# Five of sixteen key and value steps projected in earlier stages, a key scratch with all 96 rows of each head, stores issued by the sync engine

## The chip, the cores and the metric

The kernel runs on one core of a Trainium2 chip. Its engines are PE (TensorE, the matrix engine, with PEld for its weight loads), DVE (VectorE), ACT (ScalarE), POOL (GpSimd) and SP (SyncE, which here only issues transfers). Each engine runs its own list of instructions in order and waits on semaphores for the others. The metric is the time of one execution in microseconds, as the median over several runs.

## The reference

The program is a small perceiver of two layers over a residual x of 8 x 32 = 256 tokens by 256 channels, with a context of 8 x 512 = 4096 tokens. Cut to what matters:

```python
def fq(x, axis):                       # int8 rounding in f32
    s = max(max(|x|, axis) / 127, 1e-8)
    return clip(round(x / s), -127, 127) * s

x = x + masked_attention(layernorm(x), ctx, mask)       # keys and values are ctx itself
x = x + scan(layernorm(x))                              # state space scan, 64 states
x = x + moe(layernorm(x), experts=64, top=6)            # grouped choice, and a shared expert

q = (layernorm(x) @ Wq + bq) / 4                        # 16 heads of 16 channels
k, v = split(ctx @ Wkv + bkv)                           # 4096 tokens each
q, k = fq(q, axis=channel of head), fq(k, axis=channel of head)
v = fq(v, axis=token)                                   # one scale per channel, over all tokens
p = softmax(q @ k.T)                                    # then rounded to 255 steps of its maximum
x = x + (p @ v) @ Wp + bp

x = x + gated convolution and MLP; x = x + moe(layernorm(x), experts=16, top=4)
```

## The kernel before

The program is a sequence of seven stages, each a block of the five engines' programs with a barrier behind it: first attention (`xattn0_stage`), scan, first mixture of experts (`moe0_stage`), keys and values (`kv_stage`), heads (`xattn1_stage`), convolution and MLP (`conv_stage`), second mixture (`moe_stage`). Within a stage the order of each engine is the order in which the code is written; there is no scheduler. What one engine does is released to another by a semaphore (`wait_ge`, `then_inc`).

**Keys and values.** The 4096 context tokens are taken in 16 steps of 256 (`STEPS`, `KPS` = 2 chunks of 128 tokens). For step m PE makes two halves, keys and values: each four f32 matmuls of 128x256 (L1683) and two short ones (L1685) that add the bias, held in three bf16 parts. DVE quantizes the keys per head in five operations (L1505 to L1512). ACT and POOL split the f32 result exactly into three bf16 parts (L1620, L1577, L1624, L1580). Two steps later PE turns the 3 x 2 x 2 blocks of 128x128 (L1698), ACT copies the turned keys from PSUM to one of two buffers `k_kT` (L1610) and issues their store to a scratch in HBM (L1614). ACT also copies the values (L1599) and their absolute values (L1602), of which DVE keeps a running maximum (L1540), which POOL reduces over the partitions at the end. SP loads the context of each step into one of two slots as soon as PE has projected the step two back (L1366), and at the end begins the loads of the keys of heads 0 and 1. The queries are projected, quantized and split in the same stage, between the steps.

The copy of turned keys waits for the store that last left the same buffer:

```python
def copy_turned(m):
    act.wait_ge(kT_psum, m + 1)
    if m >= 2:
        act.wait_ge(kT_stored[m % 2], m // 2 * 16)
```

**The scratch and the heads.** The product of queries and keys is made exactly from six products of parts (`PRODUCTS`), so each head's keys stand as 6 x 16 = 96 rows in SBUF (`kst`). The scratch holds the three parts once (3 x 256 rows). Each head's 96 rows are read from it by six transfers of 16 rows, since a part that is in several products is read several times (`load_keys`, L1373). Heads 0 and 1 are loaded in pieces: the first 12 steps, the steps 12 to 14 (`LATE`), and the last step straight from SBUF (`last_keys`). In the head stage PE multiplies (L2068), DVE takes the maximum (L1913), ACT the exponential (L2009), POOL rounds (L1895), and PE turns and multiplies by the values (L2095, L2111).

**The stages around.** In the first attention PE turns the normalized tokens, makes the scores in two halves (L281), turns the exponentials (L287) and multiplies by the context (L296). The first mixture gathers the tokens of four experts at a time with matmuls (L1033), runs them through (L1048, L1060, L1069, L1081) and adds them back (L1091), 16 groups in a pipelined loop; four slots hold the experts' weights, two of them (`w0_early`) loaded during the first attention. There the bias of keys and values is split into parts too (L959, L853). `keep_warm` (L122) is a helper of matmuls whose result nobody reads.

## Time and profile before

| | us |
|---|---|
| runs | 713.3, 715.14, 716.4 |
| median | 715.14 |
| profiled execution | 715.68 |
| its span | 713.6 |
| first attention | 33.5 |
| scan | 133.3 |
| first mixture | 118.4 |
| keys and values | 88.3 |
| heads | 213.9 |
| convolution and second mixture | 126.2 |

The profiled execution is 715.68 us long, of which the span of instructions is 713.6 us. Over the span PE is busy for 86%, DVE 67%, ACT 55% and POOL 37% of the time, and the mean granted clock of TensorE is 0.916 of full. These shares are averages over stages with different limits, so each stage is read by itself, in the windows of the rows below. A row of the timeline has the start, the duration and the engine; what stands in square brackets is how long the engine had been idle and what released it. Of transfers the issue is on the queue of an engine (SPq, ACTq), and the landing is told from the issue.

### The profile page before, as it was taken

To read this page: it belongs to the slowest core of one execution; us is meant where nothing else is said; L and a number is where in the kernel's file an instruction comes from. 1 tells how busy PE (TensorE), PEld (TensorE's weight loads), DVE (VectorE), ACT (ScalarE), POOL (GpSimd) and SP (SyncE) were. 2 spreads that over 40 slices of the span, in tenths; PEclk is the share of its full clock that TensorE was granted. 3 is DMA by queue.
4 is the path that set the end of the run, shared out by engine and by line. 5 is a ranking of instruction groups with operands and counts; after the bars stand their busy time and mean duration, and the time that the engine had idled before them with its cause. 6 is when DMAs were issued, how large, how long until landed. Compare 5 with 4: busy or idle time off the path is not lost. (4 is left out here: it accounts for less than half of the span.)

```text
span 713.6 us, 12686 instructions
## 1 busy us (share of the span) xinstructions
PE 612.9 (86%) x4694; PEld 403.5 (57%) x4694; DVE 480.9 (67%) x762; ACT 393.8 (55%) x759; POOL 331.7 (46%) x263
## 2 busy tenths in 40 slices
PE   3767999994899999989965788888898879989996
PEld 1333445443677776877741445554555566657775
DVE  3358999995543323778977799999899945333222
ACT  1237965533222222568867799999899943122221
POOL 1039999992111110244634778888788920000000
PEclk9988999999799999999995598889768879999999
DMA  8918300005166660144463969797898639700000
GB/s 345 337 49 326 125 0 1 0 0 177 59 200 198 200 200 1 56 123 142 132 177 97 191 127 164 150 169 142 160 153 143 126 62 410 300 1 1 0 0 15
DMA packets 97802, 93.84 MB, mean 132 GB/s; under 512 B 70673, under 2 KB 88657, under 8 KB 93585
## 3 DMA queue, kind: packets, MB, share of 16 engines
q1 hardware_dynamic: 85072, 86.72, 45.6%
q10 hardware_dynamic: 12672, 6.36, 3.1%
q8 instruction: 36, 0.59, 0.3%
q14 instruction: 22, 0.17, 0.1%
HBM read 69.56 MB, written 6.62 MB: 107 GB/s over the span
## 5 line engine op out<-in xcount | busy, mean ns | idle before, releaser
L1913 DVE TENSOR_REDUCE d_nmax<-d_psum 128x1 f32<-128x1024 f32 x128 | 152.1, 1214 | 7.9 <-PE d_psum L2068 7.7
L2068 PE MATMUL d_psum<-kst,qT 96*128 96x512 bf16 x256 | 97.2, 476 | 31.3 <-ACT d_e L2009 11.8
L426 POOL TENSOR_TENSOR b_h<-b_h,b_cb 128x1024 f32<-128x1024 f32 x32 | 87.7, 2740 | 6.8 <-DVE b_h L476 6.0
L1895 POOL TENSOR_SCALAR d_rounded<-d_e,d_lift 128x1024 f16<-128x1024 f32 x64 | 72.4, 1132 | 21.2 <-ACT d_lift L2013 14.4
L2009 ACT ACTIVATE d_e<-d_psum,d_nmax 128x1024 f32<-128x1024 f32 x64 | 71.3, 1119 | 17.4 <-DVE d_nmax L1913 16.7
L1895 POOL TENSOR_SCALAR d_rounded<-w_early,d_lift 128x1024 f16<-128x1024 f32 x62 | 70.1, 1131 | 17.3 <-ACT d_lift L2013 13.1
L476 DVE TENSOR_TENSOR_SCAN b_h<-b_dA,b_psum 128x1024 f32<-128x1024 f32 x32 | 73.2, 2286 | 2.5 <-ACT b_dA L531 2.0
L531 ACT ACTIVATE b_dA<-b_dtT,b_A 128x248 f32<-128x248 f32 x128 | 53.7, 490 | 33.1 <-DVE b_h L476 28.1
L2009 ACT ACTIVATE w_early<-d_psum,d_nmax 128x1024 f32<-128x1024 f32 x64 | 71.4, 1121 | 0.1
L1683 PE MATMUL k_psum<-k_wkv,k_ctxT 128*128 128x256 f32 x256 | 64.1, 381 | 1.4 <-PEq L812 1.4
L2095 PEld LDWEIGHTS d_psum<-d_ident_f,d_rounded 128*128 128x128 f16 x512 | 43.2, 119 | 32.6 <-issue 20.1
L587 PE MATMUL b_psum<-b_bdiag,b_dtx 128*128 128x512 f32 x128 | 60.2, 594 | 0.8 <-DVE b_h L476 0.8
L2095 PE MATMUL d_psum<-d_ident_f,d_rounded 128*128 128x128 f16 x512 | 50.4, 257 | 6.2 <-ACT d_probsT L2021 3.1
L2068 PEld LDWEIGHTS d_psum<-kst,qT 96*128 96x128 bf16 x256 | 19.8, 110 | 59.6 <-ACT d_e L2009 20.9
L1683 PEld LDWEIGHTS k_psum<-k_wkv,k_ctxT 128*128 128x128 f32 x256 | 43.5, 190 | 11.1 <-issue 1.8
L2111 PEld LDWEIGHTS d_psum<-d_vh,d_probsT 128*128 128x128 f16 x1024 | 43.5, 98 | 9.7 <-issue 5.5
L847 POOL TENSOR_TENSOR c_pick_weighed<-c_pick,c_w 128x384 f32<-128x384 bf16 x16 | 13.4, 838 | 76.2 <-PE c_psum L1069 70.2
L2111 PE MATMUL d_psum<-d_vh,d_probsT 128*128 128x16 f16 x1024 | 43.9, 171 | 2.3 <-issue 1.6
L608 PE MATMUL b_psum<-b_h,ident 128*128 128x256 f32 x128 | 36.1, 404 | 6.9 <-DVE b_h L483 4.4
L608 PEld LDWEIGHTS b_psum<-b_h,ident 128*128 128x128 f32 x128 | 21.8, 189 | 33.8 <-DVE b_h L483 32.2
L1272 PE MATMUL f_psum<-w,f_xnT 128*128 (+1 forms) x128 | 40.5, 459 | 0.0
L883 DVE TENSOR_TENSOR c_a<-c_silu,c_psum 128x192 f32<-128x192 f32 x16 | 5.7, 355 | 51.0 <-ACT c_silu L947 51.0
(398 smaller groups left out, 1177.2 us busy)
## 6 DMA issues: line engine op xcount, KB each, us to landing
kst<-kT_scratch SPq DMA_DIRECT2D x84, 128.0 KB, 3.0
w<-in_w SPq DMA_DIRECT2D x8, 1088.0 KB, 19.3
b_cb<-c_scratch SPq DMA_DIRECT2D x4, 2048.0 KB, 7.1
w_early<-in_w0gu SPq DMA_DIRECT2D x8, 768.0 KB, 5.0
w_late<-in_w0gu SPq DMA_DIRECT2D x8, 768.0 KB, 4.9
kT_scratch<-k_kT ACTq DMA_DIRECT2D x15, 384.0 KB, 2.7
a_ctxT<-in_ctxT SPq DMA_DIRECT2D x2, 2048.0 KB, 12.2
a_ctx<-in_ctx SPq DMA_DIRECT2D x2, 2048.0 KB, 20.7
```

The lines of the kernel that those rows point to most:

```text
L426: nc.gpsimd.tensor_tensor(hv, hv, cv, ALU.mult).then_inc(hc_ready, 1)
L476: nc.vector.tensor_tensor_scan(h[s][:, :], dA[s % 2][:, :], ps[:, 2 * (s % 2):2 * (s % 2) + 2, :] .rearrange("p a b -> p (a b)"), 0.0, ALU ...
L531: nc.scalar.activation(out[:, :, j, :, 1:L], src, ACT.Exp, scale=A[:, c, n * NT + j:n * NT + j + 1]).then_inc(dA_ready, 1)
L587: last = nc.tensor.matmul(ps[:, 2 * (s % 2) + t, :], dtx[:, t, c * P:(c + 1) * P], bdiag[t][:, n * NT:n * NT + NT, :], start=True, stop=True)
L608: last = nc.tensor.matmul(ps[:, 4 + c, 0:T], ident[:, :], hv[:, j], start=False, stop=False, skip_group_check=True)
L1683: nc.tensor.matmul(psum_kv(m, part)[:, j, :], cT[m % 2][:, k, j * P:(j + 1) * P], wkv[:, k, cols], start=(k == 0), stop=False)
L1895: nc.gpsimd.tensor_scalar(tile_of(r, j), e[j], lift[t][:, f:f + 1], HALF_ULP_ONE, ALU.mult, ALU.add).then_inc(r_ready, 1)
L1913: nc.vector.tensor_reduce(nm[:, t, m:m + 1, f:f + 1], quarter(m, j).unsqueeze(1), AX.X, ALU.max, negate=True).then_inc(nm_ready, 1)
L2009: nc.scalar.activation(e[j].unsqueeze(1), quarter(m, j).unsqueeze(1), ACT.Exp, bias=nm[:, t, m:m + 1, f], accum_out=zp[:, t, m:m + 1, f]). ...
L2068: last = nc.tensor.matmul(quarter(m, j)[:, b * 512:(b + 1) * 512], qT[0:QROWS, m:m + 1, t * P:(t + 1) * P], kst[m % 2][0:QROWS, at:at + 51 ...
L2095: last = nc.tensor.transpose(turn_tile(m, j)[:, b * P:(b + 1) * P], tile_of(r, j)[:, b * P:(b + 1) * P], ident16[:, :])
L2111: last = nc.tensor.matmul(out, pT[m % 2][:, t, b, :], vh[m % 2][:, b, :], start=(b == 0), stop=(b == NKC - 1 and t not in BY_DMA))
```

## The change

**Projected ahead.** Steps 0 to 4 of keys and values (ten halves) are projected before their stage: five halves in the first attention and five in the first mixture. ACT copies each from PSUM to SBUF (`keep_half`). To that end the weights `wkv` are loaded second in the program, the context of these steps ahead of the rest, and the bias is split at the very start of the first attention, by POOL, ACT and DVE. In the loop of the first mixture DVE quantizes the five key steps, ACT and POOL split them, and DVE takes the values' maximum so far. The weights of the first mixture's experts are now all loaded at its own start, since the memory of the two early slots (`spare`) holds the early keys, values and `wkv`.

**The key and value stage** has 11 steps (5 to 15), three slots for the context and five for the split parts. `TURNS` says which turns stand in which pass of the loop; those of the early steps are doubled up with the later ones. The absolute copies of the values are gone; DVE takes the maximum from the values themselves, every second step, and POOL's reduction over the partitions moves to the head stage, with the value scale after it.

**The scratch** holds all 96 rows of each head, so the parts are written as often as they are used: a step's store is six transfers (768 KB) in place of one (384 KB), and SP issues them. A head's keys are one transfer of 96 rows (768 KB).

**Smaller edits.** Fewer `keep_warm` matmuls (28 to 19 and 12 to 3 in the convolution stage, 17 to 14 in the second mixture, 5 to 0 in the first, whose place the projections take); in the convolution stage the products are released one by one, the two kinds of silu alternate, and the gates follow two convolutions behind.

```diff
+EARLY_PROJECTED = 5
+FIRST_HALVES = ((0, 0), (0, 1), (1, 0), (1, 1), (2, 0))
+SECOND_HALVES = ((2, 1), (3, 0), (3, 1), (4, 0), (4, 1))
...
+def keep_half(nc, act, g, n, bank):
...
+    act.wait_ge(g["early_psum"], n + 1)
+    nc.scalar.activation(dst, bank.rearrange("p (c n) -> p c n", n=D), ACT.Copy).then_inc(g["early_read"], 1)
...
                 step = Steps(dve, chain)
+                dve.wait_ge(bkv_in, 16)
+                for q in range(K_PARTS):
+                    src = ([bkv] + bias_rest)[q]
+                    nc.vector.tensor_copy(bias_part[q][:, :], src[:, :]).then_inc(bias_part_ready, 1)
+                    if q < K_PARTS - 1:
+                        dve.wait_ge(bias_part_ready, q + 1)
+                        step(nc.vector.tensor_tensor(bias_rest[q][:, :], src[:, :], bias_part[q][:, :], ALU.subtract))
                 dve.wait_ge(g["x_in"], 16)
                 ln.vector(dve, step, xn, x, xn_ready)
...
+STORED_ROWS = ((0, 3), (3, 2), (5, 1))
+STORED = 16 * len(STORED_ROWS) * KC
...
+def store_keys(queue, g, src, done, cols):
+
+    dst = g["kT_store"][:, :, :, cols]
+    parts = src[:, :, :].rearrange("p (q k) n -> p q k n", q=K_PARTS)
+    for first, count in STORED_ROWS:
+        for k in range(KC):
+            queue.dma_start(dst[:, first:first + count, k, :], parts[:, 0:count, k, :]).then_inc(done, 16)
+
+
+def load_keys(queue, d, dst, done, head, cols):
+
+    queue.dma_start(dst[0:QROWS, cols], d["kT_scratch"][head * QROWS:(head + 1) * QROWS, cols]).then_inc(done, 16)
...
+TURNS = ((0,), (), (1, 2), (3, 4), (5,), (6, 7), (8, 9), (10,), (11,), (12,), (13,))
+QUERY_PARTS = (5, 7, 9)
...
             @block.sync
             def _(sp):
-                for m in range(2, STEPS):
-                    sp.wait_ge(v_psum, m - 1)
-                    load_context(sp, d, g, m)
+                def store(m):
+                    sp.wait_ge(kT_ready, m + 1)
+                    store_keys(sp, g, kT[slot(m)], kT_stored[slot(m)], slice(m * KEYS, (m + 1) * KEYS))
+
+                for i in range(STEPS - FIRST):
+                    m = FIRST + CTX_SLOTS - 1 + i
+                    if FIRST + CTX_SLOTS <= m < STEPS:
+                        sp.wait_ge(v_psum, nth(m - CTX_SLOTS))
+                    if m < STEPS:
+                        load_context(sp, d, g, m)
+                    if i:
+                        for u in TURNS[i - 1]:
+                            store(u)
...
                 for h in range(2):
                     load_keys(sp, d, g["kst"][h], g["k_early"][h], h, EARLY)
+                for m in (LAST - 1, LAST):
+                    store(m)
...
                 def copy_turned(m):
 
                     act.wait_ge(kT_psum, m + 1)
                     if m >= 2:
-                        act.wait_ge(kT_stored[m % 2], m // 2 * 16)
+                        act.wait_ge(kT_stored[m % 2], m // 2 * STORED)
...
+                for i in range(STEPS - FIRST):
+                    if i:
+                        copy_values(FIRST + i - 1)
+                    split0(FIRST + i)
+                    for m in TURNS[i][0:1]:
+                        copy_turned(m)
+                    split1(FIRST + i)
+                    for m in TURNS[i][1:]:
+                        copy_turned(m)
+                    if i in QUERY_PARTS:
+                        query_part(QUERY_PARTS.index(i))
+                copy_values(LAST)
...
+                for i in range(STEPS - FIRST):
+                    keys(FIRST + i)
...
+                    for m in TURNS[i]:
+                        turn(m)
+                    if i:
+                        values(FIRST + i - 1)
+                values(LAST)
                 turn(LAST - 1)
```

How the instructions stand now is shown at three places. First SP in the key and value stage. Before, `k_v_psum` (the values of a step are in PSUM) releases one context load after the other, and behind the last the loads of the keys:

```order
L812 UNCONDITIONAL_BRANCH
L1480 UNCONDITIONAL_BRANCH [waits barrier_Pool_Activation_PE_DVE_SP_release]
L1366 DMA k_ctxT<-in_ctxT 128x2x256 [waits k_v_psum] x14
L1373 DMA kst<-kT_scratch 16x3072 [waits kT_stored1,kT_stored0]
L1373 DMA kst<-kT_scratch 16x3072 x11
```

Now, in the passes of the loop around the turns 3 and 4, the stores of two steps stand between two context loads (`k_kT_ready` is the copy of turned keys):

```order
L1541 DMA k_ctxT<-in_ctxT 128x2x256 [waits k_v_psum]
L1555 DMA kT_scratch<-k_kT 128x3x256 [waits k_kT_ready]
L1555 DMA kT_scratch<-k_kT 128x3x256
L1555 DMA kT_scratch<-k_kT 128x2x256 x2
L1555 DMA kT_scratch<-k_kT 128x256 x2
L1555 DMA kT_scratch<-k_kT 128x3x256 [waits k_kT_ready]
L1555 DMA kT_scratch<-k_kT 128x3x256
L1555 DMA kT_scratch<-k_kT 128x2x256 x2
L1555 DMA kT_scratch<-k_kT 128x256 x2
L1541 DMA k_ctxT<-in_ctxT 128x2x256 [waits k_v_psum]
```

The stores have moved from ACT to SP, behind a context load and its wait for the values. The second place is ACT in one pass of the same stage. Before:

```order
L1620 ACTIVATE k_parts<-k_kq 128x512 [waits k_kT_psum,k_kq_ready]
L1599 ACTIVATE v<-k_psum 128x512 [waits k_v_psum]
L1602 ACTIVATE k_v_abs<-k_psum 128x512 [waits k_vrun_ready]
L1610 ACTIVATE k_kT<-k_psum 128x1536 [waits kT_stored0,k_kT_psum]
L1624 ACTIVATE k_parts<-k_rest 128x512 [waits k_rest_ready]
L1614 DMA kT_scratch<-k_kT 128x6x256 [waits k_kT_ready]
L1620 ACTIVATE k_parts<-k_kq 128x512 [waits k_kT_psum,k_kq_ready]
```

And now one and a half passes, of which the first has two copies of turned keys (L1810), each with its wait for a store of its own buffer (`kT_stored0`, `kT_stored1`):

```order
L1803 ACTIVATE v<-k_psum 128x512 [waits k_v_psum]
L1816 ACTIVATE k_parts<-k_kq 128x512 [waits k_kq_ready]
L1810 ACTIVATE k_kT<-k_psum 128x1536 [waits kT_stored1,k_kT_psum]
L1820 ACTIVATE k_parts<-k_rest 128x512 [waits k_rest_ready]
L1810 ACTIVATE k_kT<-k_psum 128x1536 [waits kT_stored0,k_kT_psum]
L1803 ACTIVATE v<-k_psum 128x512 [waits k_v_psum]
L1816 ACTIVATE k_parts<-k_kq 128x512 [waits k_kq_ready]
L1810 ACTIVATE k_kT<-k_psum 128x1536 [waits kT_stored1,k_kT_psum]
L1820 ACTIVATE k_parts<-k_rest 128x512 [waits k_rest_ready]
```

The issue of the store and the absolute copy are gone, and a second copy of turned keys has come into the pass. The third place is PE at the program's start. Before, it turns the normalized tokens (`a_xn`) and makes the scores:

```order
L114 MATMUL a_psum<-ident,a_xn 128x128 [waits a_xn_ready,constants_ready]
L114 MATMUL a_psum<-ident,a_xn 128x128 x3
L281 MATMUL a_psum<-a_ctxT,a_xnT 32x512 [waits a_ctxT_in0,a_xnT_ready]
L281 MATMUL a_psum<-a_ctxT,a_xnT 32x512 x7
L281 MATMUL a_psum<-a_ctxT,a_xnT 32x512 [waits a_ctxT_in1]
L281 MATMUL a_psum<-a_ctxT,a_xnT 32x512 x7
```

Now a half of keys stands ahead of the transposes and two halves behind them (L137 and L138, with `spare` the memory of `wkv`):

```order
L137 MATMUL a_psum<-spare,a_ctxT 128x256 [waits k_wkv_in,a_first_ctxT_in0,k_bias_ready,constants_ready]
L137 MATMUL a_psum<-spare,a_ctxT 128x256
L138 MATMUL a_psum<-k_bias_rows,ones_bf 128x256
L137 MATMUL a_psum<-spare,a_ctxT 128x256 x2
L138 MATMUL a_psum<-k_bias_rows,ones_bf 128x256
L120 MATMUL a_psum<-ident,a_xn 128x128 [waits a_xn_ready]
L120 MATMUL a_psum<-ident,a_xn 128x128 x3
L137 MATMUL a_psum<-spare,a_ctxT 128x256 x2
L138 MATMUL a_psum<-k_bias_rows,ones_bf 128x256
L137 MATMUL a_psum<-spare,a_ctxT 128x256 x2
L138 MATMUL a_psum<-k_bias_rows,ones_bf 128x256
L137 MATMUL a_psum<-spare,a_ctxT 128x256 [waits k_early_read,a_first_ctxT_in1]
```

The scores (L281 before) come behind three halves, and the first instruction waits for the bias parts (`k_bias_ready`) and the weights (`k_wkv_in`) too.

## Rows read from the trace of the kernel before

**Rows 1.** Windows by stage: busy us of each engine (instructions), granted clock, DMA share, GB/s

```profile
core 0: us, PE busy (x) PEld busy (x) DVE busy (x) ACT busy (x) POOL busy (x), PEclk, DMA share, GB/s
0.00:33.50 33.50, 17.75 (x108) 7.73 (x109) 10.73 (x26) 6.10 (x11) 1.90 (x13) 0.95 0.93 350
33.50:166.80 133.30, 115.27 (x353) 58.86 (x353) 115.38 (x111) 75.94 (x190) 106.92 (x44) 0.96 0.19 71
166.80:285.20 118.40, 108.86 (x844) 80.90 (x844) 49.30 (x137) 29.28 (x65) 19.28 (x29) 0.96 0.50 156
285.20:373.50 88.30, 79.50 (x544) 63.69 (x544) 71.39 (x111) 64.39 (x87) 40.62 (x34) 0.99 0.43 124
373.50:587.40 213.90, 174.66 (x2332) 109.00 (x2333) 191.69 (x269) 186.34 (x328) 162.87 (x143) 0.78 0.77 142
587.40:713.60 126.20, 116.90 (x513) 83.29 (x513) 42.40 (x109) 31.73 (x81) 0.11 (x1) 1.00 0.25 103
```

**Rows 2.** Groups of the key and value stage: busy, mean ns, idle before

```profile
L1683 PE MATMUL k_psum<-k_wkv,k_ctxT 128*128 128x256 f32 x256 | 64.1, 381 | 1.4 <-PEq L812 1.4
L1698 PE MATMUL k_psum<-ident_bf,k_parts 128*128 128x128 bf16 x192 | 13.4, 219 | 6.5 <-POOL k_parts L1580 4.4 <-DVE k_parts L1566 1.9
L1610 ACT ACTIVATE k_kT<-k_psum 128x1536 bf16<-128x1536 bf16 x14 | 20.3, 1452 | 2.1 <-PE k_psum L1698 2.1
L1638 ACT ACTIVATE qs<-k_q_rest 128x1024 bf16<-128x1024 f32 x1 | 2.0, 1987 | 0.0
```

**Rows 3.** Timeline of PE, one step: start, duration, instruction

```profile
358.75 0.84 PE L1698 MATMUL k_psum<-ident_bf,k_parts 128*128 128x128 bf16 x12
363.39 0.83 PE L1698 MATMUL k_psum<-ident_bf,k_parts 128*128 128x128 bf16 x12
```

**Rows 4.** Store and context load by source line: duration ns, issue to landing

```profile
L1614 ACTq DMA_DIRECT2D kT_scratch<-k_kT x15: 366/366/406, 301.7 to 369.8; - x15
DMA to landing us min/median/max: 2.7/2.7/3.3
L1366 SPq DMA_DIRECT2D k_ctxT<-in_ctxT x16: 539/540/634, 171.8 to 353.6; - x16
```

**Rows 5.** DMA issues, first attention: KB, us to landing

```profile
b_cols<-in_cols SPq DMA_DIRECT2D x1, 4.0 KB, 2.4
```

**Rows 6.** Timeline of PE in the first mixture

```profile
179.23 0.23 PE L1010 MATMUL c_psum<-c_selb,before_bf 128*128 128x64 bf16 x1 [4.86 <-DVE c_selb L708]
183.59 2.08 PE L1033 MATMUL c_psum<-c_pick,c_xn_part 128*128 128x192 bf16 x12 [0.30 <-ACT c_gatheredT L941]
188.72 1.16 PE L1033 MATMUL c_psum<-c_pick,c_xn_part 128*128 128x192 bf16 x12
```

**Rows 7.** Windows in the first mixture and in the first attention

```profile
177.00:178.00 1.00, 0.00 (x0) 0.00 (x0) 0.86 (x5) 0.00 (x0) 0.00 (x0) 0.50 1.08 363
24.00:25.50 1.50, 1.50 (x10) 0.66 (x8) 0.00 (x0) 0.00 (x0) 0.00 (x0) 0.50 0.90 372
186.00:277.00 91.00, 91.00 (x748) 67.91 (x744) 33.16 (x70) 21.89 (x53) 13.83 (x16) 0.99 0.50 157
```

**Rows 8.** Timeline in the first attention, DVE and PE

```profile
15.84 0.69 DVE L242 SCALAR_TENSOR_TENSOR a_scores<-a_psum,a_mask 128x512 f32<-128x512 f32 x1 [6.54 <-PE a_psum L281]
22.57 9.80 PE L296 MATMUL a_psum<-a_ctx,a_expT 128*32 128x256 f32 x64
```

**Rows 9.** Timeline of PE where the heads begin

```profile
379.99 1.04 PE L2068 MATMUL d_psum<-kst,qT 96*128 96x512 bf16 x4 [1.87 <-DMA kst<-kT_scratch]
403.52 1.89 PE L2068 MATMUL d_psum<-kst,qT 96*128 96x512 bf16 x4 [3.79 <-DMA kst<-kT_scratch]
```

**Rows 10.** Timeline in the convolution stage, DVE and PE

```profile
591.95 0.69 DVE L2161 TENSOR_TENSOR e_hn<-e_y,e_ss 128x512 f32<-128x512 f32 x1
593.47 0.60 PE L114 MATMUL e_psum<-ident,e_hn 128*128 128x128 f32 x4
602.90 0.43 DVE L2229 TENSOR_TENSOR e_gated<-e_sx,e_sz 128x256 f32<-128x256 f32 x1 [2.03 <-ACT e_sx L2282]
```

580 lines of the change are left out of this document (346 added, 234 removed).

## The prediction

> **What bounds the kernel now.** I read the views in this order. First the windows by stage [rows 1]: the span of 713.6 us falls into seven stages, with a barrier between each two. PE is busy for 79.5 of the 88.3 us of the key and value stage (285.2 to 373.5) and for 108.86 of 118.4 us of the first mixture of experts. The head stage (373.5 to 587.4) is different: DVE is busy 191.69 and ACT 186.34 of its 213.9 us, PE 174.66. So work that moves off PE in the key stage shortens that stage, the same work laid on PE in the mixture lengthens it, and the heads go faster only where they wait for keys.
>
> Second, the groups of instructions of the key stage [rows 2] and one of its steps on PE [rows 3]. In a step PE does eight f32 matmuls of 0.38 us for keys and values, some short ones for their bias, and one turn. Turn to turn that takes 363.39 - 358.75 = 4.64 us: one turn of three key parts at 0.84 us and two halves (keys, values) at (4.64 - 0.84) / 2 = 1.90 us each. Third, its queues [rows 4]: a store of a step's turned keys (384 KB, one transfer, issued by ACT in 0.37 us) lands 2.7 us later, and SP needs 0.54 us to issue a context load. Fourth, PE's idle stretches and the granted clock. Last, the small waits at the edges of the other stages.
>
> **Key and value stage.** Five of 16 steps go. What goes on PE is ten halves; their five turns stay: 5 x (4.64 - 0.84) = 19.0 us. Two things come back. The last step's keys are stored by six issues of SP at 0.54 us in place of one of 0.37 us at the stage's end: +2.9. Three query copies of ACT, up to 2.0 us each [rows 2], now lie in a stage of 11 steps with as many 1.45 us copies of turned keys as before; I put 1.0 us of them on the path. That leaves -15.1 us, if nothing new is waited for.
>
> Something is. The turned keys have two buffers, so the copy of step m waits until the store of step m-2 has landed. Before, ACT issued that store right behind its copy, a whole step ahead of need. Now SP issues it, and in front of it in SP's program stands a context load that waits for the values of the same loop pass. That event is also the one with which ACT begins the pass in which it makes the next copy. So for passes whose stores were not issued earlier (the four that end with turns 3 and 4, 5, 6 and 7, 8 and 9, each followed by the turn that needs them), one loop from values to values is: context issue 0.54, store, copy 1.45, turn 0.84, values 1.90. In words: PE's turn m waits for the copy of m-2, that for the store of m-4, that for SP, and SP for PE's values.
>
> The store is now six issues of 64 to 192 KB, 768 KB in all. No row shows six such stores. From above: six at SP's 0.54 us, the last landing after the 2.7 us of a 384 KB store, 5 x 0.54 + 2.7 = 5.4 us. From below: a pitch of ACT's 0.37 us and a landing of 2.4 us, that of a 4 KB load [rows 5], 5 x 0.37 + 2.4 = 4.2 us. I take 4.5, nearer to the low end, since the issue of a store is the 0.37 us row, and the last piece is small. The loop is then 0.54 + 4.5 + 1.45 + 0.84 + 1.90 = 9.2 us. PE's own work in it is 4.64 us with one turn and 4.64 + 0.84 = 5.48 us with two: two passes of either kind, so 2 x 4.6 + 2 x 3.7 = +16.6 us (bounds +15.4 and +20.2 with the store at 4.2 and 5.4).
>
> The Trainium skill, "DMA: Bandwidth & Descriptors", section "Anatomy of one DMA", says that the fixed part of a DMA, about 2.0 us, is mostly the receipt of the write, and is the longest where the target is HBM. By that rule as an estimate, the six transfers would share one fixed part, 2.0 us plus the issue of the last, and the loop would be some 0.4 us shorter. The page is for the path of another queue, and no row of this trace splits a landing in two.
>
> Each of the four passes now holds a stretch in which PE waits: from the end of the keys (1.90 us into the loop) to the copy (6.5 us in), 4.6 us. The rows at 179 us show what such a stretch does: PE had been idle for 4.86 us when it started at 179.23 [rows 6], and the granted clock was 0.50 already at 177 us [rows 7]; that is the 1.2 GHz level. At 183.59 twelve gather matmuls still took 2.08 us, and at 188.72 twelve took 1.16 us. So after an idle of 4.86 us the halved clock outlives it by at least 6.4 us of work (179.23 to 185.67). In the loop, turn and values (2.74 us) would take 5.48 us. If all four passes lose this it is +11.0 us, if none it is 0. I take +6.5, since the first stall starts at full clock and PE fills part of the rest with slower keys that nothing waits for.
>
> The Trainium skill, "TensorE: Matmul & The Clock Gate", section "HAM oscillation — how this bites in real kernels", tells of loops in which a wait longer than the tile's work throttles the engine again in each tile, so that each starts cold. By that rule the whole +11.0 would be paid, and it speaks against this change; [rows 6, 7] agree with the drop behind one idle stretch, while no row of this trace shows it four times in a row.
>
> Sum of the stage: -15.1 + 16.6 + 6.5 = +8.0 us. Its bounds are -15.1 and, with the long store and all four at the half rate, -15.1 + 20.2 + 11.0 = +16.1.
>
> **First attention.** Five halves come in, 5 x 1.90 = 9.5 us of PE. Ahead of them stands a chain that did not exist: a small load (2.4 us to land, [rows 5]), then on DVE three casts and two subtractions of 512 columns, 0.69 us for such an operation [rows 8], and three ACT copies of a row. DVE does them before the LayerNorm, and PE starts behind them. That moves the first scores by about 3 us. Most of the other halves lie in waits that PE has there, for loads, exponentials and copies. Against it: the values matmuls of this stage, 9.80 us for 64 from 22.57 [rows 8], run partly at a granted clock of 0.50 (24.0 to 25.5, [rows 7]), and a PE that has worked in the gaps before them can win up to 2 us. I take +2.0 (bounds 0 and +5).
>
> **First mixture.** It is PE bound: 91.0 of 91.0 us busy from 186 to 277 [rows 7]. The half in its loop costs its full 1.9 us, and the two in front of the transposes delay the logits by about 0.8. Two halves go into the idle stretch of 4.86 us [rows 6], behind which the clock was halved: two gathers of 2.08 us against 1.16 give 1.8 us back, and slower matmuls beside them another 0.7. DVE is busy in 33.16, ACT in 21.89 and POOL in 13.83 of those 91 us, so quantizing, splitting and subtracting five steps hides there. Rounded up for the zeros matmul that now stands behind the shared expert: +0.6 (bounds -1.5 and +3).
>
> **Heads.** PE waited 1.87 us at 379.99 and 3.79 us at 403.52 for keys [rows 9]; the second is the load of head 2, issued as six transfers behind the many small ones of heads 0 and 1. With one transfer per head SP is free some 5 us earlier, and most of the 3.79 goes. The first is partly replaced by the wait of heads 0 and 1 for stores that now end later. The value scale moves into head 0. I take -4 (bounds -6, which is nearly all of both waits and a little later, and +1). The other heads run at the pace of DVE and do not change.
>
> **Convolution and last mixture.** In before, the normalized rows were ready at 591.95 + 0.69 = 592.64, but warming matmuls held PE until 593.47: -0.8. DVE waited 2.03 us until 602.90 for the first gate [rows 10], and the convolutions now run two ahead of the gates; half of it counts, as PE waits for gates too: -1.0. With fewer warming matmuls the clock may fall in the gap: +0.6. Together -1.2 (bounds -3, +2); fewer warming matmuls at the last stage's start, -0.4.
>
> **Sum.** The scan does not change. 715.68 + 2.0 + 0.6 + 8.0 - 4.0 - 1.2 - 0.4 = 720.7 us against the profiled execution. That one lies 0.54 us above the median of the runs, 715.14 us, so I forecast 720.
>
> **Rivals.** (A) The store comes back sooner than SP's rows say. Its six parts are small, and the place is the same loop: if the last lands 2.0 us after SP goes on, the loop is 6.7 us, the stall 2 x 2.1 + 2 x 1.2 = 6.6 us, PE's idle stretches are 2.1 us, and I let the clock stay at 2.4 GHz. The stage is then -15.1 + 6.6 = -8.5 and the time 720 - 8.0 - 8.5 = 703.5 us. It decides from a store below 3 us. For it: 384 KB in one transfer lands in 2.7. Against it: 768 KB and six issues. 0.17; faster. (B) The stores are waited for as I say, but the clock does not fall: 720 - 6.5 = 713.5 us. For it: each stall has work on both sides. Against it: [rows 6]. 0.25. (C) Forecast: 720, own range 715 to 726: 0.43. (D) The clock stays at half from the first stall to the end of the stage, keys too: the +11.0 in full and 4 x 1.9 us for keys where PE no longer idles enough, of which I put half on the path: 720 + 4.5 + 3.8 = 728, up to 733 with the long store. 0.15. That the change does not remove the five steps is no case: the order shows it.
>
> **Numbers.** A change of 0.5% (3.6 us) is what a measurement of this kernel can tell from none, so "same" is 711.6 to 718.7. Faster: all of A, 0.10 of B (gains in the heads at their bound), 0.03 of C: 0.30. Same: 0.13 of B, 0.06 of C: 0.19. Slower: the rest of C, 0.02 of B and D: 0.51. The range 703 to 729 leaves out 0.08 below and 0.08 above.
>
> **What the profile after would show.** The stage of keys and values 92 to 100 us long, with four waits of PE's turns of 4 to 5 us each ended by ACT's copy, whose own wait is ended by a DMA of the scratch; a granted clock of 0.50 behind them. First attention 35 to 36 us, first mixture 118 to 120 us without an idle stretch of PE above 3 us, heads about 210 us. I am wrong if the copies of turned keys wait less than 2 us for stores, or if those waits are there and the clock stays at 1.00.

## The result and the profile after

| | before | after |
|---|---|---|
| median of the runs | 715.0 (4 runs) | 736.04 (4 runs) |
| span of the profiled execution | 713.6 | 734.8 |
| first attention | 33.5 | 36.2 |
| scan | 133.3 | 133.3 |
| first mixture | 118.4 | 119.7 |
| keys and values | 88.3 | 105.5 |
| heads | 213.9 | 213.6 |
| convolution | 42.2 | 42.4 |
| second mixture | 84.0 | 84.1 |

The changed kernel is slower: 1.0302 times the time before, with a 95% interval of 1.0248 to 1.0357. The forecast was 720 us with a range up to 729; the sign was right, the size was not. The windows of the kernel after, of the key and value stage and of the heads, answer to [rows 1] (busy us of each engine with instructions, granted clock, DMA share, GB/s):

```profile
core 0: us, PE busy (x) PEld busy (x) DVE busy (x) ACT busy (x) POOL busy (x), PEclk, DMA share, GB/s
...
289.20:394.70 105.50, 70.22 (x443) 55.65 (x443) 49.49 (x89) 48.23 (x56) 25.82 (x22) 0.84 0.53 150
394.70:608.30 213.60, 176.50 (x2332) 113.99 (x2332) 193.26 (x271) 187.06 (x327) 163.56 (x144) 0.77 0.78 142
```

PE did 70.22 us of work in the key and value stage, 9.3 less than before, and the stage became 17.2 us longer. The granted clock fell there from 0.99 to 0.84. The heads did not become shorter. Most of the loss beyond the forecast lies in these two stages.

PE's timeline in the pass with turn 5 is the first of four of its kind, and shows what takes the place of [rows 3]:

```profile
313.58 0.27 PE L138 MATMUL k_psum<-k_bias_rows,ones_bf 96*128 96x256 bf16 x1
319.17 1.44 PE L1883 MATMUL k_psum<-ident_bf,k_parts 128*128 128x128 bf16 x12 [5.32 <-ACT k_kT L1810]
320.40 2.02 PE L137 MATMUL k_psum<-spare,k_ctxT 128*128 128x256 f32 x4
```

PE ends the keys at 313.85 us and idles for 5.32 us; then the turn takes 1.44 us (0.84 before) and the first four matmuls of the values 2.02 us (1.03 at full clock). ACT in the same pass shows what PE waited for:

```profile
311.94 0.60 ACT L1803 ACTIVATE v<-k_psum 128x512 f32<-128x512 f32 x1 [2.94 <-PE k_psum L138]
...
317.57 1.45 ACT L1810 ACTIVATE k_kT<-k_psum 128x1536 bf16<-128x1536 bf16 x1 [4.52 <-DMA kT_scratch<-k_kT]
```

ACT copies the values as soon as they are there, splits, and then waits until the store of two steps before has landed, 5.6 us after the values (311.94 to 317.57). The six transfers of that store took 5.0 us from the first issue (312.52) to the landing of the last, which came 2.1 us behind its own issue. Over the stage the waits of ACT and of PE in that circle add up (engine and line waited for, us in total, times, longest):

```profile
ACT k_kT L1810 <- DMA kT_scratch<-k_kT: 22.8, 7, 4.6
PE k_psum L1883 <- ACT k_kT L1810: 21.3, 7, 5.4
```

The second half of the loss is at the end of the stage. PE's last turn, the last copy of turned keys (by DVE) and SP's stores there:

```profile
383.22 0.84 PE L1883 MATMUL k_psum<-ident_bf,k_parts 128*128 128x128 bf16 x12
```

```profile
385.12 0.96 DVE L1756 COPY k_kT_last<-k_psum 128x1536 bf16<-128x1536 bf16 x1
```

```profile
312.52 6.73 SPq L1555 DMA_DIRECT2D kT_scratch<-k_kT  x12
...
368.89 16.28 SPq L1555 DMA_DIRECT2D kT_scratch<-k_kT  x24
...
386.16 4.35 SPq L1555 DMA_DIRECT2D kT_scratch<-k_kT  x6
390.56 3.76 SPq L1555 DMA_DIRECT2D kT_scratch<-k_kT_last  x6
```

PE's last turn had ended at 384.06 us, 10.85 us before PE's first instruction in the next stage, and the last copy at 386.08; SP issues stores up to 394.3. In the kernel before the last copy of turned keys ended at 372.3 and the stage at 373.5, 1.2 us later; here it is 8.6 us later, for a queue. PE's last turn there, 2.2 us before the end of the stage:

```profile
370.46 0.84 PE L1698 MATMUL k_psum<-ident_bf,k_parts 128*128 128x128 bf16 x12 [1.89 <-DVE k_parts L1566]
```

This is a matter of the end and not of the whole stage, as SP's own waits show (for copies of turned keys, from 288 us to the end of the stage):

```profile
SPq L1555 <- ACT k_kT L1810: 3.0, 2, 1.9
```

The row of 24 stores from 368.89 us hides these two waits: SP had caught up, and issued the stores of steps 12 and 13 as soon as ACT had copied their keys (the latter at 381.86). Behind that copy stand 20 issues, the six stores of each of the steps 13, 14 and 15 and two loads of keys, and they take 12.5 us, while PE needs only 2.2 more. The six stores of a step, by their source line (answer to [rows 4]):

```profile
L1555 SPq DMA_DIRECT2D kT_scratch<-k_kT x90: 370/493/915, 299.9 to 390.0; - x90
...
DMA to landing us min/median/max: 1.6/2.4/6.5
```

The median issue takes 0.49 us, but they follow each other at 0.56 to 0.62 us where SP doesn't wait (6.73 us for 12, 12.5 for the last 20), where the prediction had 0.54, and 0.37 as its lower bound.

### The profile page after: what moved, and what is told of

Its sections match the earlier page's. It is cut to its first block and busy times, and to the rows that moved or that the text cites. A ratio compares the mean times of both kernels' runs of the same rounds, so it can differ in the third digit from the quotient of the medians.

```text
span 734.8 us, 12653 instructions
## 1 busy us (share of the span) xinstructions
PE 618.0 (84%) x4667; PEld 413.8 (56%) x4667; DVE 481.4 (66%) x776; ACT 389.0 (53%) x746; POOL 328.3 (45%) x263
## 5 line engine op out<-in xcount | busy, mean ns | idle before, releaser
L2261 PE MATMUL d_psum<-kst,qT 96*128 96x512 bf16 x256 | 98.9, 484 | 40.9 <-ACT d_e L2202 18.8
L2089 POOL TENSOR_SCALAR d_rounded<-spare,d_lift 128x1024 f16<-128x1024 f32 x62 | 70.1, 1131 | 18.3 <-ACT d_lift L2206 14.1
L2202 ACT ACTIVATE spare<-d_psum,d_nmax 128x1024 f32<-128x1024 f32 x64 | 71.3, 1118 | 1.6 <-DVE d_nmax L2109 1.6
L2288 PEld LDWEIGHTS d_psum<-d_ident_f,d_rounded 128*128 128x128 f16 x512 | 48.9, 129 | 31.5 <-issue 23.7
L2288 PE MATMUL d_psum<-d_ident_f,d_rounded 128*128 128x128 f16 x512 | 55.5, 274 | 3.4 <-POOL d_rounded L2089 2.2
L137 PE MATMUL k_psum<-spare,k_ctxT 128*128 128x256 f32 x176 | 52.2, 432 | 1.4 <-PEq L931 1.4
L2304 PEld LDWEIGHTS d_psum<-d_vh,d_probsT 128*128 128x128 f16 x1024 | 42.4, 96 | 7.6 <-issue 2.1
L137 PEld LDWEIGHTS k_psum<-spare,k_ctxT 128*128 128x128 f32 x176 | 35.1, 221 | 10.3 <-issue 4.0
L1445 PE MATMUL f_psum<-w,f_xnT 128*128 (+1 forms) x128 | 40.5, 460 | 0.0
L1377 DVE TENSOR_TENSOR f_prod<-f_silu,f_psum 128x352 f32<-128x352 f32 x16 | 8.3, 522 | 42.2 <-ACT f_silu L1416 42.2
```

The source lines that it names most:

```text
L137: nc.tensor.matmul(out[:, j, :], ctxT[:, k, j * P:(j + 1) * P], g["wkv"][:, k, cols], start=(k == 0), stop=False)
L1445: last = nc.tensor.matmul(GU[t][u][:, 0:width], xnT[:, k, t * P:(t + 1) * P], parts[u][:, k, :], start=(k == 0), stop=(k == KC - 1))
L2089: nc.gpsimd.tensor_scalar(tile_of(r, j), e[j], lift[t][:, f:f + 1], HALF_ULP_ONE, ALU.mult, ALU.add).then_inc(r_ready, 1)
L2202: nc.scalar.activation(e[j].unsqueeze(1), quarter(m, j).unsqueeze(1), ACT.Exp, bias=nm[:, t, m:m + 1, f], accum_out=zp[:, t, m:m + 1, f]). ...
L2261: last = nc.tensor.matmul(quarter(m, j)[:, b * 512:(b + 1) * 512], qT[0:QROWS, m:m + 1, t * P:(t + 1) * P], kst[m % 2][0:QROWS, at:at + 51 ...
L2288: last = nc.tensor.transpose(turn_tile(m, j)[:, b * P:(b + 1) * P], tile_of(r, j)[:, b * P:(b + 1) * P], ident16[:, :])
```

## The experiments

All are compared with runs of the kernel before on the same chip, so that each ratio has its own time before (715.0 to 716.6 us). The stage lengths are those of the profiled execution of each.

| run | time | ratio to before (95%) | keys, values | heads |
|---|---|---|---|---|
| changed kernel | 736.0 | 1.030 (1.025 to 1.036) | 105.5 | 213.6 |
| stores ahead of the context wait | 712.5 | 0.993 (0.991 to 0.996) | 81.8 | 214.0 |
| four buffers | 710.9 | 0.995 (0.992 to 0.997) | 82.2 | 212.3 |
| projected ahead, scratch as before | 696.5 | 0.972 (0.969 to 0.975) | 70.1 | 213.6 |
| scratch alone, on the kernel before | 716.8 | 1.000 (0.997 to 1.003) | 96.4 | 207.1 |
| PE kept warm in the stalls | 727.9 | 1.019 (1.014 to 1.024) | 96.8 | 210.0 |
| value scale back | 728.7 | 1.019 (1.013 to 1.024) | 104.6 | 206.6 |
| convolution warmed as before | 736.1 | 1.028 (1.022 to 1.033) | 105.7 | 212.8 |
| projected ahead, with both repairs | 700.8 | 0.984 (0.976 to 0.991) | 72.2 | 212.6 |
| stores split between SP and ACT | 712.9 | 0.996 (0.992 to 0.999) | 89.5 | 209.3 |
| three loads per head | 816.0 | 1.139 (1.133 to 1.146) | 90.7 | 308.0 |
| three loads, rows outermost | 706.7 | 0.986 (0.982 to 0.989) | 71.1 | 215.1 |
| the same, scale in the heads | 707.6 | 0.986 (0.981 to 0.990) | 73.5 | 219.1 |

**Is the wait behind the values the cause?** In the changed kernel, the stores go ahead of the context wait and load of the same pass:

```diff
+                    if i:
+                        for u in TURNS[i - 1]:
+                            store(u)
                     m = FIRST + CTX_SLOTS - 1 + i
                     if FIRST + CTX_SLOTS <= m < STEPS:
                         sp.wait_ge(v_psum, nth(m - CTX_SLOTS))
                     if m < STEPS:
                         load_context(sp, d, g, m)
-                    if i:
-                        for u in TURNS[i - 1]:
-                            store(u)
```

> The changed kernel, with SP's stores of turned keys issued ahead of the context load (and its wait for the values) of the same pass, and nothing else. Theory 1 (the copy of turned keys waits for a store that stands behind a wait for PE's own values): the loop from values to values is broken. What is left is copy to store to copy, about 5.1 + 1.45 us for every second turn, and SP's 6 x 0.61 us for each store. The four idle stretches of PE of 3.8 to 5.4 us shrink to under 2 us, the clock stays at 1.00 there, the key and value stage falls from 106 to about 86 us, the time from 736 to about 716 us. Rival (the store itself is too slow for two buffers, wherever it is issued): the idle stretches stay above 3 us, the stage stays above 98 us, the time above 728 us.

712.5 us: 23.6 below the changed kernel, the stage 23.7 us shorter. The same two waits as above, in this kernel:

```profile
PE k_psum L1883 <- ACT k_kT L1810: 6.5, 7, 1.9
...
ACT k_kT L1810 <- DMA kT_scratch<-k_kT: 3.6, 2, 1.8
```

And SP's waits for copies of turned keys in it:

```profile
SPq L1555 <- ACT k_kT L1810: 16.4, 7, 7.5
```

ACT's waits for stores went from 22.8 to 3.6 us, PE's from 21.3 to 6.5. Theory 1 holds, and the time lies 3.5 us below what it expected. But the stage is 11.7 us longer than with single stores (70.1, below), though ACT's copies stall PE for no more than 1.9 us at a time. SP is not short of time over the stage: it stands idle for 16.4 us, waiting for copies. Its last such wait ends with the copy of step 13 at 360.11 us, PE's last turn ends at 362.30, and SP issues until 372.2.

**Is it the number of buffers?** The changed kernel with four buffers:

```diff
-        kT = [sb(f"k_kT{s}", [P, K_PARTS * KC, KEYS], BF16) for s in range(2)] + [g["kT_last"]]
+        kT = [sb(f"k_kT{s}", [P, K_PARTS * KC, KEYS], BF16) for s in range(4)] + [g["kT_last"]]
...
-                    if m >= 2:
-                        act.wait_ge(kT_stored[m % 2], m // 2 * STORED)
+                    if m >= 4:
+                        act.wait_ge(kT_stored[m % 4], m // 4 * STORED)
```

> The changed kernel with four buffers for turned keys in place of two, so that a copy waits for the store of four steps before. Theory 1: ACT's waits for the scratch's DMA (22.8 us) go, PE no longer idles between keys and values, the clock stays at 1.00. Theory 2 (96 store issues of SP at about 0.6 us are a bound of their own): SP then has some 64 us of issues from the first store on, so PE ends its last turn well before SP ends, and the key and value stage is about 81 us, not 73; the time is about 711 us. If SP's issues are no bound, the stage is 73 to 75 us and the time 704 us. If the wait for the buffer isn't the cause of the stalls, 736 us.

710.9 us, stage 82.2 us, as theory 1 and 2 together expected (711 and 81), and not the 704 of theory 1 alone. Either edit breaks the circle, and both end at nearly the same length of the stage, so what is left is not the circle. PE's last turn in this run, and SP behind it:

```profile
360.03 0.83 PE L1883 MATMUL k_psum<-ident_bf,k_parts 128*128 128x128 bf16 x12
```

```profile
348.34 13.88 SPq L1555 DMA_DIRECT2D kT_scratch<-k_kT  x24
...
363.25 4.22 SPq L1555 DMA_DIRECT2D kT_scratch<-k_kT  x6
367.52 3.88 SPq L1555 DMA_DIRECT2D kT_scratch<-k_kT_last  x6
371.81 2.49 SPq L1566 DMA_DIRECT2D kst<-k_kT_last  x4
```

PE has ended at 360.9 us; SP still issues stores until 371.4, and with that the stage ends. In this run SP hardly waits for copies (0.5 us in all), so by itself it fits theory 2, 96 issues as a limit of their own. The run before doesn't: with 16.4 us of idle time its stage ends no later. What the two have in common is the end: from the copy of step 13 to the last store it is 12.1 us there and 12.9 here, as it is 12.5 in the changed kernel.

**The five steps alone.** The changed kernel with the scratch of before: three parts once, one store per step by ACT, six loads per head:

```diff
-STORED = 16 * len(STORED_ROWS) * KC
+STORED = 16
...
+                    for m in TURNS[i][0:1]:
+                        store(m)
                     for m in TURNS[i][1:]:
                         copy_turned(m)
+                        store(m)
```

> The changed kernel with the scratch as before: three parts once, one store of 384 KB per step issued by ACT right behind its copy, six transfers of 16 rows for each head. The five steps stay projected ahead, and the other edits stay. Theory 1 and 2 both: no stall above 2.5 us in the key and value stage, its length about 75 us; the heads lose the single transfer, so PE waits for the keys of head 2 again (about 4 us): time about 708 us. Rival (doubled turns or the early projections themselves slow the stage): the stage stays above 85 us and the time above 718 us.

696.5 us, 0.972 of the time before, 11.5 us below what I expected. The stage's window, and PE's last turn:

```profile
288.20:358.30 70.10, 59.72 (x443) 48.19 (x443) 52.48 (x89) 48.33 (x57) 26.08 (x23) 1.00 0.48 136
```

```profile
354.51 0.84 PE L1884 MATMUL k_psum<-ident_bf,k_parts 128*128 128x128 bf16 x12 [1.08 <-DVE k_parts L1765]
```

At a full clock, 70.1 us: the five steps are worth 18.2 us, and the early halves cost 3.4 us in the first attention and nothing in the first mixture in this run. The last turn ends 67.2 us into the stage and the stage 2.9 us later; in the two kernels that broke the circle it was 71.5 and 71.3 us, and then 10.3 and 11.0. So of the 12 us between them some 4 are small waits of PE before its last turn, and 7.4 to 8 are the queue behind it. This is the fastest kernel of the study, faster than before and after.

**The scratch alone.** On the kernel before, with SP's store of a step four steps behind the context load:

```diff
                 for m in range(2, STEPS):
                     sp.wait_ge(v_psum, m - 1)
                     load_context(sp, d, g, m)
+                    if m >= 4:
+                        store(m - 4)
...
-    for j in rows:
-        queue.dma_start(dst[j:QROWS:len(PRODUCTS), cols], parts[PRODUCTS[j][1], head * HD:(head + 1) * HD, cols])\
-             .then_inc(done, 16)
+    queue.dma_start(dst[0:QROWS, cols], d["kT_scratch"][head * QROWS:(head + 1) * QROWS, cols]).then_inc(done, 16)
```

> The kernel before with only the scratch of 96 rows: SP issues six stores per step behind the context load (a step's store four steps behind the load), and a head's keys are one transfer. Here a store is issued two steps ahead of the copy that waits for it, 9.3 us, so theory 1 has no stall in the loop. Theory 2: SP needs 6 x 0.6 + 0.57 = 4.2 us of a step of 4.9, which fits, but the last four steps' stores stand at the end: stage +5 to +9 us. Heads 4 us shorter or the same. Time 716 to 721 us. Rival (the 768 KB stores themselves slow the stage, by the bytes they move): the stage is longer by 15 us or more, time above 728 us.

716.8 us, no difference from before (0.997 to 1.003). The stage is 8.1 us longer, inside the 5 to 9 expected of SP's issues, and the heads are 6.8 us shorter. Where each store is issued two steps ahead of need there is no circle: the last turn comes 1.6 us later in the stage than before, and the stage ends 8.6 us behind it in place of 2.2. From the copy of step 13 to the last store it is 12.0 us again. The single load per head pays this back.

**What does the clock cost?** Warming matmuls in front of the last turn of the four passes:

```diff
                     for m in TURNS[i]:
+                        if i in WARM and m == TURNS[i][-1]:
+                            pe.wait_ge(v_copied, i - 2)
+                            keep_warm(nc, g, ps[:, 2 * ((FIRST + i - 1) % 2) + 1, :], WARM[i])
                         turn(m)
```

> The changed kernel with 22, 19, 16 and 22 warming matmuls of PE (result read by nobody) in front of the last turn of the four passes in which PE idled 5.3, 4.6, 3.8 and 5.4 us. The stores are waited for as before; only what PE does meanwhile changes. Theory (the halved clock behind each stall costs turn and values 2.4 to 2.7 us more): the granted clock is 1.00 through the loop, a loop is 9.6 us in place of 12.0 to 12.7, the key and value stage 96 to 98 us in place of 106, the time about 727 us. Rival (the clock costs nothing, since slower matmuls only fill waits): stage and time unchanged, 736 us.

727.9 us. The four passes in the window of the changed kernel and of this one, and PE's timeline in this one:

```profile
311.90:361.00 49.10, 29.42 (x154) 22.98 (x154) 17.12 (x29) 18.55 (x21) 10.57 (x9) 0.76 0.47 134
```

```profile
312.70:353.00 40.30, 37.34 (x230) 23.72 (x230) 17.14 (x29) 17.98 (x20) 10.12 (x9) 1.00 0.57 164
```

```profile
314.47 4.91 PE L128 MATMUL k_psum<-ones_bf,ident_bf 128*128 128x512 bf16 x22
320.24 0.83 PE L1884 MATMUL k_psum<-ident_bf,k_parts 128*128 128x128 bf16 x12 [0.86 <-ACT k_kT L1811]
...
330.35 0.83 PE L1884 MATMUL k_psum<-ident_bf,k_parts 128*128 128x128 bf16 x12 [0.54 <-ACT k_kT L1811]
...
350.52 0.83 PE L1884 MATMUL k_psum<-ident_bf,k_parts 128*128 128x128 bf16 x12 [0.54 <-ACT k_kT L1811]
```

The granted clock is 1.00 in place of 0.76, the four passes take 40.3 us in place of 49.1, and the stage is 8.7 us shorter. That is the price of the clock here, 2.2 us for each of the four stalls. A pass is 10.1 us (320.24 to 330.35, and to 350.52 in three), so the circle itself is 10.1 us, not 9.2: the six stores, 5.0 us in place of 4.5, make 0.5 us of the difference.

**Where did the gain of the heads go?** The value reduction and the value scale back to where they were:

```diff
+                dve.wait_ge(v_copied, nth(LAST))
+                values_max(nc, step, v, vstep[:, :], LAST, STEPS)
...
+                pool.wait_ge(vam_ready, 1)
+                nc.gpsimd.partition_all_reduce(g["vall"][:, :], vam[:, :], P, RMAX).then_inc(g["vall_ready"], 1)
...
-                        if m == 0 and j == 5:
-                            value_scale()
...
+                value_scale()
                 rounds(vector_head)
```

> The changed kernel with the last maximum of the values and POOL's reduction over the partitions back at the end of the key and value stage, and the value scale back at the start of the head stage, as in the kernel before. Theory (the predicted gain of 4 us in the heads was eaten by the reduction at their start, after which POOL's first rounding came 15.1 us into the stage in place of 10.0): POOL begins to round about 10 us into the stage again, the heads are 4 to 5 us shorter (209 us), the key and value stage as long as it is, since SP is later than all others there; time 731 to 732 us. Rival (one transfer per head gains nothing): heads 213 to 214 us, time 736 us.

728.7 us, and the heads 7.0 us shorter. POOL and DVE at the start of the heads, in the changed kernel (the two rows of POOLq, the sequencer of POOL, are from the views by source line, with first and last start in us; `MODIFY_POOL_CONFIG` stands ahead of the reduction and ahead of the first rounding):

```profile
L2063 POOLq MODIFY_POOL_CONFIG  x2: 11/11/11, 394.9 to 394.9; - x2
L2089 POOLq MODIFY_POOL_CONFIG  x2: 98/98/98, 401.7 to 401.7; - x2
```

```profile
400.55 1.16 POOL L2063 PARTITION_ALL_REDUCE v_absmax<-v_own_max  x1 [5.62 <-ACT d_e L2202]
409.76 4.73 POOL L2089 TENSOR_SCALAR d_rounded<-d_e,d_lift 128x1024 f16<-128x1024 f32 x4 [8.06 <-ACT spare L2202]
414.57 1.25 POOL L2071 TENSOR_TENSOR d_vh_scaled<-v,d_v_rscale 128x512 f32<-128x512 f32 x1
```

```profile
404.70 1.75 DVE L2104 RECIPROCAL d_v_rscale<-d_v_scale 128x256 f32<-128x256 f32 x1
...
415.85 0.43 DVE L2134 TENSOR_SCALAR d_vh<-d_vh_scaled 128x512 f16<-128x512 f32 x1 [7.00 <-POOL d_vh_scaled L2071]
```

and in this run:

```profile
402.05 4.74 POOL L2092 TENSOR_SCALAR d_rounded<-d_e,d_lift 128x1024 f16<-128x1024 f32 x4 [9.76 <-ACT d_lift L2206]
```

```profile
408.15 0.43 DVE L2135 TENSOR_SCALAR d_vh<-d_vh_scaled 128x512 f16<-128x512 f32 x1 [2.57 <-POOL d_vh_scaled L2074]
```

The head stage begins at 394.7 in the one and at 392.1 in the other. POOL's first rounding comes 15.0 us into the stage in the changed kernel and 10.0 us here; DVE idles 7.00 us for the scaled values of head 1 in the one and 2.57 in the other. POOL's record of the reduction is only 1.16 us long and ends at 401.7, 2 us before the lift is ready, so by the lengths of the records it should have been free. The rows of the sequencer say where the rest is: POOL is configured anew at 394.9 for the reduction, which starts 5.7 us later though its input was ready at 396.0, and again at 401.7 for the rounding, which starts 8.1 us later. In the six other runs with the reduction in the heads this last stretch is 6.8 to 7.7 us. With the reduction in the key stage the first of the two stands there, where POOL idles anyway, and the second at the start of the heads, under the 9.8 us in which POOL waits for the lift. What POOL does in these stretches no record tells, and that they are the cause is read from the order of the rows; that the loss goes when the reduction leaves the stage is shown.

**The convolution.** Twelve warming matmuls again behind the projection:

```diff
-                keep_warm(nc, g, ps[:, 5, :], 3)
+                keep_warm(nc, g, ps[:, 5, :], 12)
```

> The changed kernel with twelve warming matmuls in place of three behind the projection in the convolution stage, as before the change. There 12 matmuls of the output projection took 4.54 us, in the kernel before 8 took 1.99. Theory: with the warming matmuls the clock stays full, the convolution stage is 1.5 to 2 us shorter (40.5 us in place of 42.4), the time 734 us. Rival: the stage stays at 42.4 us, or is longer since the warming matmuls stand in front of the output projection.

The output projection in the changed kernel and in this one (busy, mean ns, idle before):

```profile
L2513 PE MATMUL e_psum<-e_w_outT,e_gated 128*128 128x256 f32 x16 | 5.6, 518 | 2.6 <-DVE e_gated L2427 2.6
```

```profile
L2513 PE MATMUL e_psum<-e_w_outT,e_gated 128*128 128x256 f32 x16 | 3.9, 386 | 0.7 <-DVE e_gated L2427 0.7
```

The matmuls are back at 386 ns in place of 518, and the stage at 40.5 us. But the time does not tell: 736.1 us. Without this edit the same stage was 40.3 us in both runs that broke the circle and 43.7 us in another, so whether the clock falls there changes from kernel to kernel, and one profile proves nothing. Inconclusive.

**Both repairs on the five steps alone.**

> The scratch and its single stores by ACT as in the kernel before, the five steps projected ahead, and the repairs of the two runs before this one together: reduction of the values back in the key and value stage, value scale at the start of the heads, twelve warming matmuls in the convolution stage. From 696.5 us of the kernel that is only projected ahead: if both repairs hold here, -4 us (the heads start sooner, though here the keys of head 2 come in six transfers) and -1.5 us: 691 to 692 us. Rival: the POOL reduction now ends the key and value stage, which has no slack behind SP's stores any more, and takes 2 us of it back: 694 us or more.

700.8 us (0.976 to 0.991), not better than the 696.5 us of the kernel without repairs. The stage took 72.2 us, 2.1 more, and the heads 212.6, only 1.0 less: the rival holds. With six loads per head something else holds the heads; what, was not looked for. POOL's reduction ends only 0.5 us before the stage does here (360.30 of 360.77 us), so it has no cover once SP's stores are gone.

**Half of the issues to ACT.** Stores ahead of the context wait, four buffers, value scale back, and

```diff
+                def store(m):
+                    act.wait_ge(kT_ready, m + 1)
+                    store_keys(act, g, kT[slot(m)], kT_stored[slot(m)], slice(m * KEYS, (m + 1) * KEYS), (1,))
```

> The changed kernel with its double stores, but the three transfers of the upper 128 channels of each step issued by ACT behind its copy and the three of the lower by SP; with SP's stores ahead of the context wait, four buffers, and the value reduction and value scale back where they were. Theory 2 (with the loop broken, SP's 96 issues of 0.6 us are what ends the key and value stage: 82 us in both runs that broke the loop, against 70 us with single stores by ACT): SP has half as many issues, the stage is 72 to 75 us; with heads of about 207 us the time is 694 to 698 us. Rival (768 KB per step, not the issues, hold the stage): the stage stays near 82 us and the time at 703 us or more. If ACT's issues hold ACT up, the stage is between.

712.9 us, stage 89.5 us: worse than 82, so theory 2 had the wrong remedy. The issues by queue:

```profile
L1556 SPq DMA_DIRECT2D kT_scratch<-k_kT x45: 359/490/2265, 298.4 to 376.7; - x45
L1556 ACTq DMA_DIRECT2D kT_scratch<-k_kT x45: 394/507/2171, 298.4 to 376.0; - x45
...
DMA to landing us min/median/max: 2.3/3.1/7.2
```

An issue costs ACT as much as SP, median 0.51 against 0.49 us, not the 0.37 us of the one large store in [rows 4], and ACT's copies wait behind them; the landing went up to a median of 3.1 us. PE's last turn:

```profile
372.04 0.84 PE L1900 MATMUL k_psum<-ident_bf,k_parts 128*128 128x128 bf16 x12 [1.34 <-DVE k_parts L1775]
```

It ends 82.5 us into the stage, 11 us later than in the two runs with 82 us, and the stage ends 7.0 us behind it in place of 10.3 and 11.0; from the copy of step 13 to the last store it is 8.8 us in place of 12.1 and 12.9. So half of the issues for SP do shorten the end, and the half that ACT got costs more in the loop than that. No run moved only the stores of the last three steps.

**Three loads per head.** The rows of a head ordered by product, single stores, value scale back (the edit is shown against the six loads of the kernel before):

```diff
-    for j in rows:
-        queue.dma_start(dst[j:QROWS:len(PRODUCTS), cols], parts[PRODUCTS[j][1], head * HD:(head + 1) * HD, cols])
+    for first, count in STORED_ROWS:
+        queue.dma_start(dst[first * HD:(first + count) * HD, cols], parts[0:count, head * HD:(head + 1) * HD, cols])
```

> Single stores by ACT (three parts once), the five steps projected ahead, value reduction and value scale back, and the 96 rows of a head ordered product by product, so that a head's keys are three transfers of 48, 32 and 16 rows from the scratch of before, in place of six of 16 rows spread over every sixth partition. Theory (the heads gain by fewer issues of SP in front of the transposes that the same queue carries, 7 us with one transfer per head, with the value scale in place): most of that is to be had with three, heads 208 to 210 us, key and value stage 72 us, time 692 to 695 us. Rival (the gain of one transfer comes from its long lines or its shape): heads 212 to 213 us, time 697 to 700 us.

816.0 us, a miss for both. The heads took 308.0 us. PE's waits for keys, and the DMA line (40 slices of 406 to 416 us: busy share in tenths, then GB/s):

```profile
PE d_psum L2262 <- DMA kst<-kT_scratch: 101.8, 15, 9.3
```

```profile
DMA  1111130399920302021221201229101111015000
GB/s 33 66 66 66 66 98 33 83 258 245 123 98 33 66 33 98 33 98 66 66 66 66 98 33 66 80 84 67 66 0 66 66 66 66 0 48 51 33 33 0
```

15 waits of 6.8 us on average and 9.3 at most, with the DMA engines busy for 0.1 to 0.3 of the time in most slices. The next run only reorders the same bytes, so that 16 stand outermost, in the source and in the order of the rows in SBUF:

```diff
-        queue.dma_start(dst[first * HD:(first + count) * HD, cols], parts[0:count, head * HD:(head + 1) * HD, cols])
+        queue.dma_start(dst[first * HD:(first + count) * HD, cols],
+                        parts[0:count, head * HD:(head + 1) * HD, cols].rearrange("q c n -> c q n"))
```

> The run with three loads per head again, but with the rows of a load ordered channel by channel and the parts inside, so that each transfer has 16 in its outermost place, where the run before it had 3, 2 and 1. That one had a key load that ran at 33 to 66 GB/s and a DMA share of 0.1, with 9 us waits of PE in each head. Theory (a transfer is dealt out over the DMA engines by its outermost dimension, so 3, 2 and 1 reach few of them): the waits of 9 us go, the heads are 207 to 211 us, the key and value stage 72 us, the time 693 to 697 us. Rival (rows of 8 KB over fewer than 96 partitions are slow however they are ordered): heads above 300 us, time above 790 us.

706.7 us: the waits of 9 us are gone, and the DMA line of 402 to 412 us, also during such a load, reads

```profile
DMA  0000049999999999999000400999997919994794
GB/s 0 0 0 0 0 101 218 219 205 215 221 212 223 197 146 203 236 222 63 7 8 11 13 9 9 241 290 287 293 291 152 492 33 426 262 262 66 98 295 66
```

mostly over 200 GB/s during the load where it was mostly 33 to 98. So the shape of the transfer, not its bytes, was the 109 us. But the heads are 215.1 us, not 207 to 211, and longer than the 212.6 us with six loads: three loads now land 5.4 to 6.0 us after their issue, and PE waits 22.9 us for keys in the stage. A copy of the last, with the value scale in the heads:

> The same three loads per head, but with the value reduction and the value scale in the head stage, as the change has them. Theory: POOL's reduction at the start of the heads costs there what it costs the double scratch (7 us), and spares the key and value stage 2 us: heads 5 to 7 us longer than in the run before, stage 70 us, time 3 to 5 us above it. Rival: without stores that end late the reduction is early enough, and this run is the faster one by 2 us.

707.6 us against 706.7: the heads are 4.0 us longer, a little less than the 5 to 7 expected, but the key stage was not shorter in this run (73.5), and the times do not tell the two apart.

## Why the prediction was wrong, by its steps

- **The circle** (copy, store, context wait, values) was right: four stalls, of the turns 5, 7, 9 and 10, in the four passes foretold, of 5.32, 4.63, 3.81 and 5.42 us where 4 to 5 were predicted, ended by ACT's copy. The loop without the clock was put at 9.2 us and is 10.1; the six stores took 5.0 us in place of 4.5, between the bounds, and the other 0.4 us were not split. Stalls and clock together were put at 23.1 us; taking the circle away gave 23.7. The clock's share was put at 6.5 of a possible 11.0 and measured at 8.7. The Trainium skill, "TensorE: Matmul & The Clock Gate", section "HAM oscillation — how this bites in real kernels", says that a loop with waits longer than its work starts cold in every round. The trace agrees as to the drop, four times in a row: each turn behind a stall took 1.44 us in place of 0.84. The whole 11.0 us of that weight were not paid.
- **The failed step** is "The last step's keys are stored by six issues of SP at 0.54 us in place of one of 0.37 us at the stage's end: +2.9". It counted the issues of one step. But the copies of the last three steps come within 4.2 us, and SP's stores for them, 18, and two loads between them all stand behind the copy of step 13: 12.5 us of issues. PE's last turn ended 2.2 us before the end of the stage in the kernel before and 10.7 us in this one, which makes +8.5 in place of +2.9, and 5.6 us of the 9 that the stage missed. In the kernel that has only the new scratch it is +6.4 (8.6 us), in the one with single stores +0.7 (2.9 us).
- **The rest of the key stage**, 3.6 us, lies before the last turn: it ended 94.9 us into the stage, where the terms give 86.2 - 18.0 + 16.6 + 6.5 = 91.3. Without the circle it ended at 71.3 and 71.5, where they give 68.2, and with single stores at 67.2. So with double stores some 3 us of small waits remain that the prediction put at nothing. The query copies, which I charged with 1.0 us, may have cost up to 0.8: with single stores the stage lost 18.2 us of 19.0 possible. What the 0.8 are was not looked for.
- **The heads**, put at -4, are -0.3. Two terms were mis-sized, with opposite signs, and they don't add up one by one. With the value scale at the start of the heads, one transfer per head is worth 6.8 us (213.9 to 207.1, on the kernel before) or 6.0 (212.6 to 206.6, with the five steps ahead); with reduction and scale in the heads it is worth nothing (213.6 and 213.6). The move of reduction and scale, which I named without a price, takes 7.0 us away with one transfer per head and 1.0 with six. It costs on POOL, of which no row before showed the rounding with a reduction ahead of it. Why one transfer is worth more than the 3.79 us of the wait for head 2 stays open.
- **First attention** +2.7 (put at +2.0), **first mixture** +1.3 (put at +0.6) and the scan 0: within their bounds. The values matmuls of the first attention took 8.17 in place of 9.80 us, as expected.
- **Convolution and second mixture**, put at -1.6, are +0.3: the convolution stage started PE's first product 0.7 us sooner, and then lost more where the clock fell (0.96 over the stage in place of 1.00), which was in the bounds. Whether the clock falls there changed from kernel to kernel.
- The sum of what was missed: 9.2 us in the key stage, 3.7 in the heads, 1.9 in the convolution, 1.4 early: 16.2 us, which is the distance from 720 to 736.

Of the rivals, A and B are dead: the stores were waited for, and the clock fell. D came nearest in time (728), by a mechanism that it did not have.

## What to carry to other kernels

When stores or loads are cut into more transfers or moved to another queue, add up that queue's issues twice: over the whole stage, and behind the last events that it waits for, since those end the stage (their number times the pitch at which they follow each other, not the shortest record). With the circle broken the whole was some 58 us of 82 and left the queue 16 us of waiting, and the last 20 issues ended the stage with 12 us. A wait that stands in front of a store in the queue's program belongs to everyone who waits for the store; look for the circle. And undo each part of a mixed change alone: here one part was worth 2.8% of the time and lay hidden under two others.
